# Two-layer Mamba kernel: the x_proj results in 10 DMAs per item instead of 22, and 197 instead of 186 steps of u*B on GpSimd

## The reference

```
xr, z = split(u @ W_in)                      # 2 x 192 channels
x     = silu(causal_conv(xr, 4 taps) + b)
dt, Bm, Cm = split(x @ W_x, [6, 6 + 16])     # "x_proj": rank 6, and 16 states
delta = softplus(dt @ W_dt + b_dt)
h     = exp(delta * A) * h + (delta * x) * Bm     # per channel and state, along the sequence
y     = sum over the 16 states of h * Cm
out   = ((y + x * D) * silu(z)) @ W_out
```

## Time and profile before

| | before |
|---|---|
| median of three runs | 2138.49 us |
| profiled execution, its own time | 2146.87 us |
| its span, first to last instruction | 2144.7 us |
| POOL busy | 1914.5 us, 89% |
| PE busy | 1867.0 us, 87% |
| DVE busy | 1815.2 us, 85% |
| ACT busy | 1153.9 us, 54% |
| mean granted TensorE clock | 0.947 of full speed |
| share of the DMA engines' time in use (SP's and ACT's queue) | 64.3% |

### The profile page before, as it was taken

How to read it: one execution, slowest core, us unless ns; L and a number is a source line. 1 busy time by engine, 2 the same in 40 slices (tenths; PEclk the granted TensorE clock), 3 DMA queues, 4 the chain that set the end, 5 groups by cost and what they waited for, 6 DMA issues and landing times. The chain is left out here.

```text
span 2144.7 us, 17077 instructions
## 1 busy us (share of the span) xinstructions
PE 1867.0 (87%) x4966; PEld 691.2 (32%) x4966; DVE 1815.2 (85%) x1083; ACT 1153.9 (54%) x1182; POOL 1914.5 (89%) x842
## 2 busy tenths in 40 slices
PE   6797889798898799889889789879979988978777
PEld 2332333233243233233333233323323323322222
DVE  1888897677888988997798997898889989799994
ACT  3666465556656445644665645735565564453331
POOL 0998899896998998998799899899799999989995
PEclk8899999899999999999899989999999999999897
DMA  3667658555675765785676686676566576668673
GB/s 98 224 208 166 202 191 208 164 189 169 170 241 195 193 207 185 203 238 172 181 210 217 188 207 198 218 192 222 178 167 214 180 216 205 217 183 225 222 220 82
DMA packets 126249, 416.22 MB, mean 194 GB/s; under 512 B 20092, under 2 KB 24460, under 8 KB 126156
## 3 DMA queue, kind: packets, MB, share of 16 engines
q1 hardware_dynamic: 126012, 415.06, 64.3%
q10 hardware_dynamic: 144, 0.07, 0.0%
HBM read 404.63 MB, written 6.29 MB: 192 GB/s over the span
## 5 line engine op out<-in xcount | busy, mean ns | idle before, releaser
L898 POOL TENSOR_TENSOR ring<-ring,c_ring 128x1024 f32<-128x1024 f32 x576 | 1347.0, 2366 | 154.7 <-DMA c_ring<-c_rows 79.6
L511 PE MATMUL y_ps<-ring,wp 128*128 128x512 f32 x2304 | 1173.3, 626 | 46.9 <-DVE yv_fwd L828 18.7
L848 DVE TENSOR_TENSOR_SCAN ring<-a_ring,b_ps 128x1024 f32<-128x1024 f32 x390 | 891.5, 2286 | 32.3 <-issue 0.5
L511 PEld LDWEIGHTS y_ps<-ring,wp 128*128 128x128 f32 x2304 | 432.4, 197 | 569.1 <-issue 459.1
L848 DVE TENSOR_TENSOR_SCAN ring<-b_ps,b_ring 128x1024 f32<-128x1024 f32 x186 | 422.1, 2276 | 79.9 <-POOL b_ring L892 47.2
L495 PE MATMUL b_ps<-b_in,sel 96*64 96x512 bf16 (+1 forms) x1076 | 250.5, 406 | 177.5 <-DVE ring L848 174.3
L811 DVE TENSOR_TENSOR b_ps<-u_ab,b_ps 128x1024 f32<-128x1024 f32 x242 | 293.7, 1214 | 104.9 <-PE b_ps L495 90.4
L651 ACT ACTIVATE a_ring<-delta_ab,wp 128x1024 f32<-128x1024 f32 x242 | 273.9, 1140 | 186.4 <-DVE ring L848 178.5
L892 POOL TENSOR_TENSOR b_ring<-u_ab,b_ring 128x1024 f32<-128x1024 f32 x142 | 335.7, 2364 | 4.9 <-DMA b_ring<-b_rows 4.9
L644 ACT ACT_TABLE_LOAD x186 | 238.6, 1283 | 74.6 <-DVE ring L848 33.1
L651 ACT ACTIVATE b_ps<-delta_ab,wp 128x1024 f32<-128x1024 f32 x142 | 158.4, 1117 | 215.1 <-DVE ring L848 214.0
(11 more groups left out here) (83 smaller groups left out, 815.2 us busy)
## 6 DMA issues: line engine op xcount, KB each, us to landing
c_ring<-c_rows SPq DMA_DIRECT2D x384, 512.0 KB, 4.6
c_ring<-c_rows SPq DMA_DIRECT2D x384, 256.0 KB, 4.4
b_ring<-b_rows SPq DMA_DIRECT2D x142, 512.0 KB, 5.4
b_ring<-b_rows SPq DMA_DIRECT2D x88, 256.0 KB, 5.5
out<-io SPq DMA_DIRECT2D x16, 192.0 KB, 3.6
io<-x SPq DMA_DIRECT2D x6, 384.0 KB, 5.8
b_in<-parts SPq DMA_DIRECT2D x72, 32.0 KB, 1.8
dt_in<-parts SPq DMA_DIRECT2D x138, 12.0 KB
```

The costliest lines, as they stand in the source:

```text
L511: nc.tensor.matmul(half(y_ps[:, :], j), ident, half(ring[:, g % RING, :], j), start=(n == 0 and kind != ROWS), stop=(n == NS - 1)).then_in ...
L848: nc.vector.tensor_tensor_scan(out=h, data0=a, data1=b, initial=0.0, op0=ALU.mult, op1=ALU.add).then_inc(h_ready, 1)
L898: nc.gpsimd.tensor_tensor(r, r, c_ring[:, g % C_RING, :], ALU.mult).then_inc(g_ready, 1)
```

## The change

Two things change.

1. **The gather.** B and C are copied into one tile `bc_out` and stored in one DRAM tensor `bc_rows`; a half is one DMA in place of two. The rows of `parts3` are moved with all their parts in one DMA: the pairs of parts for dt are reordered into runs of 3, 2 and 1 (`DT_RUNS`), so that a half is three DMAs (36, 24 and 12 destination rows) in place of six, and B is one DMA of 96 rows for each half in place of three of 32. The rows of `w_dt`, `sel` and `split` are packed in the matching order. A gather is 10 DMAs in place of 22 and moves the same bytes.
2. **The tables.** `BY_POOL` names 197 steps in place of 186: item 1 has 17 (16 before), item 2 has 19 (14), items 5 and 8 have 18 (15), items 6 and 9 have 16 (17), item 10 has 14 (13); the numbers of the other items stay, with other steps in them. Some jobs stand up to two slots later, one a slot earlier.

```
-DT_TERMS = ((0, 0), (0, 1), (1, 0), (1, 1), (0, 2), (2, 0))
+DT_TERMS = ((0, 0), (1, 0), (2, 0), (0, 1), (1, 1), (0, 2))
+DT_RUNS = ((0, 3), (3, 2), (5, 1))
...
-           2: (2, 5, 8, 9, 11, 14, 16, 18, 19, 22, 23, 31, 39, 42),
+           2: (2, 4, 8, 9, 11, 12, 13, 14, 16, 17, 18, 19, 20, 22, 23, 25, 31, 39, 42),
...
-           FWD: (1, 5, 8, 9, 11, 14, 16, 17, 19, 21, 25, 30, 38, 39, 42),
+           FWD: (1, 2, 4, 7, 8, 9, 10, 14, 16, 17, 18, 21, 22, 25, 30, 38, 41, 42),
...
-        BC_LOADS, DT_LOADS = 16 * 6, 32 * len(DT_TERMS)
+        BC_LOADS, DT_LOADS = 16 * 2, 32 * len(DT_RUNS)
...
         def gather_dt(eng, kind, h):
-            for q, (g, _) in enumerate(DT_TERMS):
-                eng.dma_start(half(dt_in[2 * RANK * q:2 * RANK * (q + 1), :], h),
-                              parts3[C_AT * h + B_ROWS:C_AT * h + SPLIT_ROWS, g, :]).then_inc(K["dt_loaded"][kind], 16)
+            rows = parts3[C_AT * h + B_ROWS:C_AT * h + SPLIT_ROWS, :, :]
+            for q, n in DT_RUNS:
+                eng.dma_start(half(dt_in[2 * RANK * q:2 * RANK * (q + n), :], h),
+                              rows[:, 0:n, :]).then_inc(K["dt_loaded"][kind], 16)
...
                     for h in range(2):
-                        sp.dma_start(half(b_rows[slot].rearrange("b n t -> (b n) t"), h),
-                                     b_out[C_AT * h:C_AT * h + B_ROWS, :]).then_inc(c_kept, 16)
-                        sp.dma_start(half(c_rows[slot].rearrange("b n t -> (b n) t"), h),
-                                     c_out[C_AT * h:C_AT * h + B_ROWS, :]).then_inc(c_kept, 16)
+                        to = bc_rows[slot].rearrange("v b n t -> (b n) v t")[:, :, h * HALF:(h + 1) * HALF]
+                        sp.dma_start(to, bc_out[C_AT * h:C_AT * h + B_ROWS, :, :]).then_inc(c_kept, 16)
...
                     for h in range(2):
-                        for g in range(3):
-                            sp.dma_start(half(b_in[B_ROWS * g:B_ROWS * (g + 1), slot, :], h),
-                                         parts3[C_AT * h:C_AT * h + B_ROWS, g, :]).then_inc(K["bc_loaded"][kind], 16)
+                        sp.dma_start(half(b_in[:, slot, :], h), parts3[C_AT * h:C_AT * h + B_ROWS, :, :]).then_inc(K["bc_loaded"][kind], 16)
```

More of the change, by code:

```diff
@@ L128, in fills_post @@
     return [(s, name, kind, pair, i) for s, name, i in sorted(out, key=lambda x: x[0])]
[L134 to L137, removed]
+PREP = dict(split=(0, 1, 2, 3), xr=(0, 2, 4.5, 6.5, 8.5, 11), silu=(4, 4, 8.5, 8.5, 12.5, 12.5), skip=(14, 16, 16), dbl=(15.5, 18),
+            dt=(25, 25, 35, 35, 31, 31), u=(26, 35, 31), z=(20, 22, 24, 24, 27, 27))
+POST = {ROWS: dict(gated=(2, 2, 7.5), w_out=(13, 13, 14, 14), var=(20, 22, 23, 23, 32, 33, 33, 36),
+                   log=(25, 25, 37, 37), rstd=(26, 26, 38, 38), norm=(27, 28, 39, 40), centre=(30.5, 30.5, 32, 31),
                    affine=(42, 43)),
@@ L247, in build_program @@
         b_in = sb("b_in", [C, 2, T], bf16)
-        b_out = sb("b_out", [P, HALF])
-        c_out = sb("c_out", [P, HALF])
+        bc_out = sb("bc_out", [P, 2, HALF])
         parts3 = sb("parts3", [P, 3, HALF], bf16)
@@ L263, in build_program @@
         bank = ps("bank", [P, 2, HALF])
-        b_rows = nc.dram_tensor("b_rows", (2, 2, NS, T), f32, kind="Internal").ap()
-        c_rows = nc.dram_tensor("c_rows", (2, 2, NS, T), f32, kind="Internal").ap()
+        bc_rows = nc.dram_tensor("bc_rows", (2, 2, 2, NS, T), f32, kind="Internal").ap()
         def col(name, layer=None):
@@ L457, in look_ahead_c @@
                 if g % STEPS == 0:
-                    sp.wait_ge(c_kept, 64 * (g // STEPS + 1))
+                    sp.wait_ge(c_kept, 32 * (g // STEPS + 1))
                 wait(sp, g_ready, g - C_RING + 1)
-                spread_row(c_ring[:, g % C_RING, :], c_rows[parity(kind, pair)], k, n, c_spread[g % C_RING])
+                spread_row(c_ring[:, g % C_RING, :], bc_rows[parity(kind, pair), 1], k, n, c_spread[g % C_RING])
             def look_ahead_b(g):
@@ L471, in look_ahead_b @@
                         sp.wait_ge(h_ready, pool_steps[m - B_RING] + 1)
-                    spread_row(b_ring[:, b_slot(g), :], b_rows[parity(kind, pair)], k, n, b_spread[b_slot(g)])
+                    spread_row(b_ring[:, b_slot(g), :], bc_rows[parity(kind, pair), 0], k, n, b_spread[b_slot(g)])
             walk(SP_ORDER, job, SP_LEAD, ahead_b=look_ahead_b, ahead_c=look_ahead_c)
@@ L704, in job @@
                     src = full(unit)
-                    nc.scalar.activation(b_out[:, :], src, ACT.Copy).then_inc(K["b_cut"][kind], 1)
+                    nc.scalar.activation(bc_out[:, 0, :], src, ACT.Copy).then_inc(K["b_cut"][kind], 1)
                     nc.scalar.activation(parts3[:, 0, :], src, ACT.Copy).then_inc(K["hi_ready"][kind], 1)
                 elif name == "dbl":
-                    empty(unit, nc.scalar.activation(c_out[:, :], full(unit), ACT.Copy))
+                    empty(unit, nc.scalar.activation(bc_out[:, 1, :], full(unit), ACT.Copy))
                 elif name == "constants":
@@ L934, in pack, with put @@
     wp = np.zeros((P, NCOL), np.float32)
-    def put(name, layer, a, row=0, at=0):
+    def put(name, layer, a, row=0, at=0, step=1):
         c = _cols[name, layer][0] + at
-        wp[row:row + a.shape[0], c:c + a.shape[1]] = a
+        wp[row:row + step * a.shape[0]:step, c:c + a.shape[1]] = a
     for layer, pre in enumerate(("L0_conv_", "L1_conv_")):
@@ L952, in pack @@
                 put("w_dbl", layer, w[P:], b * DM, 2 * X_COLS + at)
-            for q in range(len(DT_TERMS)):
-                put("w_dt", layer, w_dt[:, :P], RANK * (2 * q + b), b * P)
-                put("w_dt", layer, w_dt[:, P:], RANK * (2 * q + b), 2 * P + b * DM)
+            for first, n in DT_RUNS:
+                for q in range(n):
+                    row = 2 * RANK * first + RANK * b * n + q
+                    put("w_dt", layer, w_dt[:, :P], row, b * P, n)
+                    put("w_dt", layer, w_dt[:, P:], row, 2 * P + b * DM, n)
         put("w_out", layer, w_out[:P])
@@ L970, in pack @@
             for n in range(NS):
-                sel[(g * 2 + b) * NS + n, b, n] = 1.0
+                sel[3 * (b * NS + n) + g, b, n] = 1.0
     split = np.zeros((DT_ROWS, 2), np.float32)
-    for q, (_, g) in enumerate(DT_TERMS):
-        split[2 * RANK * q:2 * RANK * (q + 1)] = (-1.0 if g >= 1 else 0.0, -1.0 if g == 2 else 0.0)
+    for first, n in DT_RUNS:
+        for q in range(n):
+            g = DT_TERMS[first + q][1]
+            split[2 * RANK * first + q:2 * RANK * (first + n):n] = (-1.0 if g >= 1 else 0.0, -1.0 if g == 2 else 0.0)
     put("centre", None, np.eye(C, dtype=np.float32) - np.full((C, C), 1.0 / C, np.float32))
```

16 lines of the change are left out of this document (8 added, 8 removed), and 4 rows, old and new, of the table BY_POOL.

## The result

The changed kernel takes 2062.82 us (median of four runs, 2061.24 to 2067.44), beside 2141.15 us for the kernel before (2137.53 to 2146.9, four runs). The ratio is 0.9635, 95% interval 0.9606 to 0.9665: faster by 3.65%. The forecast was 2071 us in a range of 2044 to 2110.

The account below looks back on a forecast made before the run. POOL was taken to set the end, held by SP's issue time in gathers. The terms sum to -67.5 us, from 2146.87 to 2079.4; less 8.4 for a slow profiled execution, the forecast is 2071 us, range 2044 to 2110.

Parts of the forecast that it names:

- The gather (-72): On SP: merged DMAs shorten a gather from 15.0 to 6.9 us, cutting POOL's waits for C rows by 72 us.
- The B row (-3): POOL's longer wait for b_ring, 2.9 us behind the gather of item 2, goes too: -3 us.
- The start (-3.5): First gather, on the serial path to the first step: fewer dt issues on SP bring -3.5 us.
- Eleven more products (+26): On POOL: eleven added products at 2.366 us each cost +26 us.
- What of it fills holes (-25): Items 1, 2, 5, 8, 10: added products fall into POOL's waits for the scan, hiding 25 us; ends 10 and 31.
- The lead that the stall gave (+10): Behind gathers: without POOL's stall DVE loses its lead, so waits for the scan cost +10 us; ends 0 and 22.
- The signs: Profile after: c_ring waits at most 10 us, scan waits 60, POOL busy near 1940, items 5 and 8 shorter by 8-10.
- The moved slots at nothing: Moved job slots, at most two steps on ACT and PE, cost nothing, lying where the tables move load anyway.
- Rival B: DVE and PE are the bound at once: 2094 us, or about 2122 with dearer DMAs; chance 0.14.
- Rival C: Items 2, 5, 8: runs of POOL steps block SP, delaying C rows, 23 us in five places: 2094 us; chance 0.10.
- D: SP's gather: a merged DMA costs as much as its parts, so waits stay: +16 us, 2154 us; chance 0.05.
- E: SP's issue is not what POOL waits for; waits stay at 79.6: +1 us, about 2139 us; chance 0.05.

Follow-up runs that it names:

- the tables alone: Kernel before with the tables and job slots of the changed one, its gather keeping 22 DMAs: 2125.41 us, ratio 0.9911.
- the gather alone: Changed kernel with BY_POOL, PREP, POST and their variants of before, so only the 10-DMA gather is new: 2088.29 us, ratio 0.9736.
- the run with the late steps: Changed kernel with items 2, 5 and 8 given the lists of before plus as many added steps, late in the item: 2093.88 us, ratio 0.9762.
- the 22 DMAs issued by two engines: Kernel before, with ACT instead of SP issuing the dt rows of the second half in every gather: 2103.12 us, ratio 0.9805.

## Why the prediction was right, point by point

- **What bounds the kernel: right.** POOL set the end and still does; its busy time and waits account for the whole change of the span.
- **The sum: too small, and the forecast came nearer than its terms.** Between the two profiled executions the forecast expected -67.5 us and the time fell by 82.8. Most of the 15 us that are missing is one step: the waits for the scan (the holes and the lead together) were put at -15 and measured -29.8. Two smaller things hid half of it: I took 8.4 us off because the profiled execution of before was the slowest of its three, and the profiled execution after lies 1.2 above its own median. This is why 2071 stands only 8 us above 2062.82.
- **The gather (-72): right, measured -74.8.** A merged DMA is issued in about the time of one part (0.635 us for 0.590, 0.776 for 0.714); the gather takes 7.2 to 7.8 us where 6.9 was forecast. Two experiments change SP's issue time, one down with the DMAs themselves unchanged and one up, and the waits follow.
- **The B row (-3): -1.9.** The 2.9 us wait behind the gather of item 2 went and so did the one at the start; two of 1.4 and 1.6 us came.
- **The start (-3.5): the first product comes 8.2 us earlier, POOL's wait at the start is 5.1 shorter.** The gather's share of the 8.2 is about 4 (3.6 to 4.9), near the forecast. Step 0 of item 0 was missing (about 1.5): POOL made the products u*B of steps 0 and 2 ahead of its first product with C, and the first scan waited for one of them; now step 0 is DVE's. It is plain in the diff of the table, and the forecast looked at its counts only. The rest, 1.7 to 2.6, was the clock of the profiled execution of before.
- **Eleven more products (+26): right, +24.7.**
- **What of it fills holes (-25): mis-sized, -41 to -52, and the one step that missed in either order.** Between the kernel before and the tables alone the waits for the scan fall by 41 us, between the gather alone and the whole change by 52 (96.6 to 45.0). I had bounded the term by 31, the added products themselves. That is a bound only if nothing but these is changed; the lists also move steps within an item, and the slots go with them. Only the slots were taken out by themselves; what the steps that moved are worth was not tried. The mechanism, POOL's work in the PE-bound first part, is confirmed by the run with the late steps.
- **The lead that the stall gave (+10): +22 with the old tables, +11 with the new ones.** With the new tables the term is as forecast. With the old ones, from whose rows it was worked out, it is at the upper end, which was worked out from the last item; 8 of the 22 lie ahead of the gathers, where that end did not look for them, so the match with 22 is partly luck.
- **Delta from ACT (no term): +4.** POOL waits 5.5 us for it in place of 1.5.
- **The signs.** The waits for C rows (4.8, none above 1.7), POOL's and DVE's busy time (1939.2, 1799.4) and item 2 (-5) came as announced. The waits for the scan were 45 and not 60, item 5 was shorter by 13 and not 8 to 10, item 8 by just under 8.
- **The moved slots at nothing: wrong,** 8 to 11 us, though only together with the new steps. The sentence that they lie where the tables move the load anyway was the reason to look, not the reason to leave them out.
- **Rival B** (DVE and PE bound at once) did not happen: POOL is at 94% and waits 45 us for the scan. The gather alone comes nearest to it, with 96.6 us of such waits, above the 90 that were to be B's sign; the tables took that away.
- **Rival C** (runs of POOL steps block SP): SP's queue waits more for scans, but POOL has no wait for a C row in items 2 and 8, and those in the other items (0, 1, 3 and 5) stand behind the gathers. The row to set beside the earlier trace rows:

```profile
SPq L443 <- DVE ring L844: 180.5, 47, 11.0
```

  45 us more of waiting on SP costs POOL one wait of 1.4 us for a B row in item 2. With the 22-DMA gather the new lists cost more there: the wait for a B row behind that item's gather was 5.9 us in the run with the tables alone, and 2.9 before. In a run of POOL steps POOL falls behind the scans, as the argument against C said, so the C row has time.
- **Rivals D and E** fell with the issue times and with the 22 DMAs issued by two engines. The Trainium skill's sentence (page "DMA: Bandwidth & Descriptors", section "Issuing engines are not separate DMA queues") that starting DMAs on several engines saves only sequencer time, which is usually small, holds here in its first half: only sequencer time was saved, and here it was worth 42 us.

## What to carry to other kernels

Where one queue both refills the buffers of the bound engine and does bulk work now and then, count the issue time of the bulk work against the rows that the bound engine still has: what it exceeds them by is paid nearly in full (0.7 to 0.9 us for each us here), and merging the issues or lending some to another engine gives it back. A stall that is removed may have given other engines a lead, so look for the wait that comes in its place and move the load at the same time. Moved work is free only in the stretches where another engine sets the pace; judge a new table by where its entries stand, and its first entry too, and not by their count.

## What the runs showed that I had not expected

- Three parts in one DMA (96 rows of 1 KB, SBUF to SBUF) are issued in 0.635 us, one part (32 rows) in 0.590. A store of 64 KB and one of 128 KB both take 0.42 us to issue. The rows cost at the landing: part 6 of the profile has the merged transfers of the changed kernel at 3.7 and 2.3 us, where they were 2.9 and 1.8 before.

```profile
bc_rows<-bc_out SPq DMA_DIRECT2D x24, 128.0 KB, 3.7
...
b_in<-parts SPq DMA_DIRECT2D x24, 96.0 KB, 2.3
```

- The granted clock fell to 0.80 from 16 to 24 us of the serial start in two of the twelve profiled executions, and made the start about 2.5 us longer; PE was busy in all of these 8 us with or without the fall, and what brought it on is open. A start that differs by a few us between two executions has to be compared by its windows first.
